# Graph attention layer: one gathered step in 26 is fetched row by row from the queues of SyncE and ScalarE

## The reference

```python
h = jnp.maximum(_layernorm(x, axis=-1), 0.0)
h = (h @ W_node.T).reshape(num_nodes, H, HD)
e = (edge_features @ W_edge.T).reshape(num_edges, H, HD)
att = jnp.sum(jnp.concatenate([h[src], h[tgt], e], axis=-1) * a, axis=-1)
att = jnp.where(att > 0, att, 0.2 * att)
m = jnp.maximum(segment_max(att, tgt), 0.0)
ex = jnp.exp(att - m[tgt])
denom = segment_sum(ex, tgt) + (num_edges - deg)[:, None] * jnp.exp(-m)
x = x + segment_sum((ex / denom[tgt])[:, :, None] * h[src], tgt).reshape(num_nodes, H * HD)
```

## Time and profile before

| | us |
|---|---|
| median of 3 runs | 4519.24 (4519.19 to 4522.25) |
| the profiled execution, its own time | 4519.71 |
| its span in the profile | 4517.7 |
| POOL busy | 3382.6 (75%) |
| DVE busy | 2492.8 (55%) |
| ACT busy | 1366.4 (30%) |
| PE busy | 819.8 (18%) |
| mean DMA rate | 139 GB/s |

### The profile page before, as it was taken

How to read it: one execution, slowest core, us unless ns; L and a number is a source line. 1 busy time by engine, 2 the same in 40 slices (tenths; PEclk the granted TensorE clock), 3 DMA queues, 4 the chain that set the end, 5 groups by cost and what they waited for, 6 DMA issues and landing times.

```text
span 4517.7 us, 21382 instructions
## 1 busy us (share of the span) xinstructions
PE 819.8 (18%) x3685; PEld 777.8 (17%) x3685; DVE 2492.8 (55%) x3230; ACT 1366.4 (30%) x1008; POOL 3382.6 (75%) x3532
## 2 busy tenths in 40 slices
PE   6301111112121211111121212121111112121200
PEld 4301111111111111111111111111111111111100
DVE  7516555555555555555555555555555555555553
ACT  8103333333333333333333333333333333333320
POOL 6777777777777777777777777777777777777756
PEclk6655555555555555555555555555555555555555
DMA  7424444444444444444444444444444444444453
GB/s 265 131 90 136 138 134 141 130 141 135 142 135 142 135 142 135 138 139 132 138 134 142 135 142 135 142 134 142 135 134 140 130 141 135 142 135 142 134 171 97
DMA packets 189542, 627.98 MB, mean 139 GB/s; under 512 B 74865, under 2 KB 75634, under 8 KB 188882
## 3 DMA queue, kind: packets, MB, share of 16 engines
q0 software_dynamic: 115936, 252.37, 23.3%
q1 hardware_dynamic: 73586, 375.40, 22.5%
HBM read 382.66 MB, written 244.86 MB: 139 GB/s over the span
## 4 chain that ended last, share of the span: by engine, by line
POOL 72%; issue 24%; DMA 1%; DVE 1%; PE 0%; POOLq 0%; ACT 0%; DVEq 0%; SPq 0%; ACTq 0%
POOL slots L291 70%; POOL tdst_scratch L294 1%; DMA V<-in_dst_dram,chunk_i 1%; POOL V L291 1%; DVE pen L448 1%; PE ae L721 0%; DVE slots L463 0%; POOL rstd L304 0%; POOLq L173 0%; DVE V L571 0%; ACT pen L364 0%; DMA rows_scratch<-slots 0%; DMA state_scratch<-R 0%; POOLq L332 0%; DVE V L581 0%
## 5 line engine op out<-in xcount | busy, mean ns | idle before, releaser
L291 POOL DMA_INDIRECT slots<-rows_scratch,idx x3224 | 3076.0, 954 | 982.4 <-issue 982.4
L732 PE MATMUL ae<-w_att,eab 128*128 128x8 f32 x3224 | 707.0, 361 | 3375.0 <-DVE z L550 3373.2
L732 PEld LDWEIGHTS ae<-w_att,eab 128*128 128x128 f32 x3224 | 696.3, 331 | 3385.8 <-DVE z L550 2433.3
L581 DVE TENSOR_TENSOR_SCAN V<-A,V 128x1848 f32<-128x1848 f32 x248 | 993.6, 4007 | 18.1
L401 ACT ACTIVATE A<-D 128x1848 f32<-128x1848 f32 x248 | 425.1, 1714 | 1849.3 <-DVE V L581 1849.3
L545 DVE TENSOR_TENSOR z<-slots,big 128x52 f32<-128x52 f32 x248 | 62.3, 251 | 1567.4 <-DMA slots<-rows_scratch,idx 1567.4
L412 ACT COPY R<-V 128x1768 f32<-128x1768 f32 x248 | 791.1, 3190 | 2.8 <-DVE V L581 2.8
L571 DVE TENSOR_TENSOR V<-slots,wexp 128x1716 f32<-128x1716 f32 x124 | 401.6, 3239 | 13.8
L571 DVE TENSOR_TENSOR V<-slots,extra 128x1716 f32<-128x1716 f32 x124 | 400.5, 3230 | 13.7
L399 ACT ACTIVATE wexp<-D 128x52 f32<-128x52 f32 x124 | 27.0, 218 | 562.5 <-DVEq L566 562.5
L399 ACT ACTIVATE extra<-D 128x52 f32<-128x52 f32 x124 | 27.0, 218 | 475.4 <-DVEq L566 475.4
(11 more groups left out here) (148 smaller groups left out, 535.2 us busy)
## 6 DMA issues: line engine op xcount, KB each, us to landing
state_scratch<-R SPq DMA_DIRECT2D x248, 884.0 KB, 4.2
eab<-in_ea_dram SPq DMA_DIRECT2D x126, 832.0 KB, 6.3
slots<-rows_scratch,idx POOLq DMA_INDIRECT x3224, 2.6
rows_scratch<-slots SPq DMA_DIRECT2D x14, 476.0 KB, 2.5
tdst_scratch<-eab SPq DMA_DIRECT2D x4, 1612.0 KB, 30.9
big<-tdst_scratch SPq DMA_DIRECT2D x8, 806.0 KB, 10.9
big<-in_x_t_dram SPq DMA_DIRECT2D x14, 448.0 KB, 8.3
big<-in_x_dram SPq DMA_DIRECT2D x7, 896.0 KB, 11.8
```

The lines of the kernel that those rows point to most:

```text
L291: pool.indirect_dma_start(buf, None, table, bass.IndirectOffsetOnAxis(ap=index, axis=0)).then_inc(done, 16)
L581: nc.vector.tensor_tensor_scan(V[:, k, 0:VAL * COL], a_all, V[:, k, 0:VAL * COL], 0.0, ALU.mult, ALU.add).then_inc(scanned, 1)
L732: last = mm(ps_ae[k][:, n * 2 * H:(n + 1) * 2 * H], eab[:, k, n * P:(n + 1) * P], w_att[:, :], start=True, stop=True)
```

## The change

In blocks with odd `q` POOL issues 12 gathers instead of 13. The 13th step's 128 rows are fetched by 128 DMAs of one row each: SP issues those for partitions 0 to 63 and ACT those for partitions 64 to 127. The node numbers lie in a new input `single`, of which a stretch for four blocks at a time is in `sidx` on one partition. An engine reads 16 of them into registers, issues 16 DMAs whose source address is worked out from a register, and so on four times. That is done for block `i + 2` in the body of block `i`, at its end: on SP after the store of block `i - 1`, on ACT after the copy of block `i - 1`; both wait for `val_done` of block `i - 2` before. Each block of the eight has a semaphore for either half, and DVE waits for both before L545. The rows for block 1 are fetched before the loop. The last body fetches rows that no block uses, and POOL waits for them before its final gathers.

```diff
+KP = KB - 1
+SPN = 64
+ACN = P - SPN
+        sidx = sb("sidx", [1, 2, SLOTS * P], i32)
+        def single_rows(eng, q, p0, n, done):
+            half, base = q // SLOTS, q % SLOTS * P
+            for a in range(p0, p0 + n, 16):
+                _, at = nc.values_load_multi_w_load_instructions(
+                    sidx[0:1, half, base + a:base + a + 16], engines=(eng.engine,), min_val=0, max_val=NP - 1,
+                    skip_runtime_bounds_check_because="node numbers of the input")
+                for j in range(16):
+                    eng.dma_start(slots[a + j:a + j + 1, q % SLOTS * KB + KP, :], rows[ds(at[j], 1), :]).then_inc(done, 16)
...
         @block.sync
+            single_rows(sp, 1, 0, SPN, row_dma_sp[1])
...
                 if not (isinstance(i, int) and i == 0):
                     store(i - 1, 1 - q % 2)
+                ahead(it, q)
+
+            def ahead(it, q):
+                a = (q + 2) % UN
+                if a % SLOTS == 0:
+                    sp.wait_ge(sidx_dma[a // SLOTS], it * 16 + (16 if q + 2 < UN else 32))
+                    sp.sem_inc(sp_rows, 1)
+                if q % 2:
+                    after(sp, val_done, it * UN + q - 1)
+                    sp.sem_inc(sp_rows, 1)
+                    single_rows(sp, a, 0, SPN, row_dma_sp[a])
+                if a % SLOTS == SLOTS - 1:
+                    sp.wait_ge(sidx_taken, it * UN + q + 1)
+                    sp.dma_start(sidx[:, a // SLOTS, :],
+                                 single[:, ds((it * 2 + (q + 2) // SLOTS) * (SLOTS * P) + 2 * SLOTS * P, SLOTS * P)]).then_inc(sidx_dma[a // SLOTS], 16)
...
         @block.gpsimd
-                for j in range(KB):
+                for j in range(KB if q % 2 == 0 else KP):
...
+            pool.wait_ge(row_dma_sp[1], (ITERS + 1) * 16 * SPN)
+            pool.wait_ge(row_dma_act[1], (ITERS + 1) * 16 * ACN)
...
         @block.scalar
                 if not (isinstance(i, int) and i == 0):
                     copy_state(i - 1, 1 - v, it, q)
+                a = (q + 2) % UN
...
+                if q % 2:
+                    after(act, val_done, i - 1)
+                    act.sem_inc(act_rows, 1)
+                    single_rows(act, a, SPN, ACN, row_dma_act[a])
+                act.sem_inc(sidx_taken, 1)
...
+            single_rows(act, 1, SPN, ACN, row_dma_act[1])
             loop(act, body)
...
         @block.vector
-                dve.wait_ge(gather_dma[s], it * (32 * KB) + 16 * KB * (q // SLOTS + 1))
+                n = KB if q % 2 == 0 else KP
+                dve.wait_ge(gather_dma[s], it * (32 * n) + 16 * n * (q // SLOTS + 1))
+                if q % 2:
+                    dve.sem_inc(block_begun, 1)
+                    dve.wait_ge(row_dma_sp[q], it * (16 * SPN) + 16 * SPN)
+                    dve.sem_inc(block_begun, 1)
+                    dve.wait_ge(row_dma_act[q], it * (16 * ACN) + 16 * ACN)
```

More of the change, by code:

```diff
@@ L32, with graph_attention_kernel @@
 RING = 8
+KP = KB - 1
+SPN = 64
+ACN = P - SPN
 PIECES = 8
 PT = T // PIECES
-def graph_attention_kernel(nc, x, x_t, src, dstf, dst16, lasts, ends, first, ea, w_node, w_node_t, a_blk, we2,
+def graph_attention_kernel(nc, x, x_t, src, dstf, dst16, lasts, ends, first, single, ea, w_node, w_node_t, a_blk, we2,
                            ident_c, centre_c, cols_c, out):
@@ L156, in graph_attention_kernel @@
         gather_dma = [sem(f"gather_dma{k}") for k in range(SLOTS)]
+        sidx_dma = [sem(f"sidx_dma{k}") for k in range(2)]
+        row_dma_sp = [sem(f"row_dma_sp{k}") for k in range(UN)]
+        row_dma_act = [sem(f"row_dma_act{k}") for k in range(UN)]
+        sidx_taken = sem("sidx_taken")
         store_dma = [sem(f"store_dma{k}") for k in range(2)]
@@ L164, in graph_attention_kernel @@
         get_dma = [sem(f"get_dma{k}") for k in range(STEPS)]
-        slots_taken = sem("slots_taken")
+        slots_taken, block_begun, act_rows, sp_rows = sem("slots_taken"), sem("block_begun"), sem("act_rows"), sem("sp_rows")
         em_done, group_done, stored = sem("em_done"), sem("group_done"), sem("stored")
@@ L239, in _ @@
             sp.dma_start(idx[:, 0, :], src[:, 0:SLOTS * KB]).then_inc(idx_dma[0], 16)
+            for k in range(2):
+                sp.dma_start(sidx[:, k, :], single[:, k * SLOTS * P:(k + 1) * SLOTS * P]).then_inc(sidx_dma[k], 16)
             for g in range(STEPS):
@@ L253, in _ @@
                 sp.dma_start(big[:, a:b], td_rows[:, a:b]).then_inc(td_dma[k], 16)
+            for k in range(2):
+                sp.wait_ge(rows_stored[k], 16 * (STEPS // 2))
+                sp.wait_ge(sidx_dma[k], 16)
+            single_rows(sp, 1, 0, SPN, row_dma_sp[1])
             state_rows = state_d[0:P * T, :].rearrange("(p t) r -> p (t r)", p=P)
@@ L264, in body @@
                     j = it * 2 + q // SLOTS
-                    after(sp, gather_dma[SLOTS - 1], j * (16 * KB))
+                    after(sp, gather_dma[SLOTS - 1], j * (16 * KP))
                     sp.dma_start(idx[:, 1 - q // SLOTS, :], src[:, ds(j * (SLOTS * KB) + SLOTS * KB, SLOTS * KB)]).then_inc(idx_dma[1 - q // SLOTS], 16)
@@ L272, in body @@
                     store(i - 1, 1 - q % 2)
+                ahead(it, q)
[12 more added lines that the diff above has]
+                                 single[:, ds((it * 2 + (q + 2) // SLOTS) * (SLOTS * P) + 2 * SLOTS * P, SLOTS * P)]).then_inc(sidx_dma[a // SLOTS], 16)
             loop(sp, body)
             store(EB - 1, 1)
+            for k in range(2):
+                sp.wait_ge(sidx_dma[k], (ITERS + 1) * 16)
             sp.wait_ge(d_ready, EB)
@@ L405, in body @@
                     copy_state(i - 1, 1 - v, it, q)
+                a = (q + 2) % UN
+                if a % SLOTS == 0:
+                    act.wait_ge(sidx_dma[a // SLOTS], it * 16 + (16 if q + 2 < UN else 32))
+                    act.sem_inc(act_rows, 1)
+                if q % 2:
+                    after(act, val_done, i - 1)
+                    act.sem_inc(act_rows, 1)
+                    single_rows(act, a, SPN, ACN, row_dma_act[a])
+                act.sem_inc(sidx_taken, 1)
             def copy_state(b, k, it, q):
@@ L412, in copy_state @@
                 nc.scalar.copy(R[:, k, :, :], vcols(k)[:, :, 1:COL].rearrange("p c t -> p t c")).then_inc(copied, 1)
+            for k in range(2):
+                act.wait_ge(rows_stored[k], 16 * (STEPS // 2))
+                act.wait_ge(sidx_dma[k], 16)
+            single_rows(act, 1, SPN, ACN, row_dma_act[1])
             loop(act, body)
@@ L777 @@
     ends[:-1, 3] = dst2[1:, 0]
+    single = _np.zeros((1, (BLOCKS + 3 * SLOTS) * P), _np.int32)
+    single[0, :BLOCKS * P] = srcp.reshape(P, BLOCKS, KB)[:, :, KB - 1].T.reshape(-1)
     eap = _np.zeros((P * T, K), f4)
@@ L791 @@
         "x": xp, "x_t": xt, "src": _np.concatenate([srcp.reshape(P, T), _np.zeros((P, SLOTS * KB), _np.int32)], axis=1), "dstf": dst2.astype(f4), "dst16": dst512.astype(_np.int16),
-        "lasts": dst512[:, -1].astype(f4).reshape(1, CL), "ends": ends, "first": dst2[:, 0:1], "ea": eat,
+        "lasts": dst512[:, -1].astype(f4).reshape(1, CL), "ends": ends, "first": dst2[:, 0:1], "single": single, "ea": eat,
         "w_node": w_node, "w_node_t": w_node.T, "a_blk": a_blk, "we2": _np.concatenate([w_edge, w_edge], axis=1),
```

## The result

The changed kernel took 6686.39 us (median of 4 runs, 6685.77 to 6698.24), the kernel before 4519.22 beside it: 1.480 times as long, 95% interval 1.4774 to 1.4825. That is 2,167 us slower. The forecast was 8,400 with a range of 6,200 to 10,500, so the side and the mechanism held and the size was 1,714 us off. L186 is the register load and L190 the row's DMA.

What follows compares the result with a forecast made beforehand. POOL bounded the kernel before, SP's ring the changed one: 355.6 us to the first scan, 123 pairs of 63.9, 58 at the end, 142 of tail and 2 around make 8417, stated as 8,400; range 6,200 to 10,500.

Steps and rivals of the forecast that it cites:

- the ring: Scan to scan through SP's queue, per pair of blocks: 5.4 + 46.4 + 2.3 + 9.8 = 63.9 us.
- The price of a row: On SP's and ACT's queues: 0.60 us per single-row DMA with address work, 38.4 us for 64.
- cheap row: Rival on the queues: a single row issues in 0.15 us, 46 us a pair, 6,200 us in all; chance 0.11.
- The register reads: Node numbers read into registers on either queue: 0.125 us each, 8 us for 64.
- The landing: After SP's last row is issued, before L545: 2.3 us until it has landed.
- What isn't rows: In SP's ring: 5.4 us from scan to the end of the store, 9.8 from L545 to the next scan's end.
- The start: Block 1's rows land at 341.8 us instead of L545 at 324.5; its scan ends at 355.6.
- the end: From the last odd ring's scan until POOL may start its final gathers: 58 us instead of 16.5.
- ACT just covered: ACT's queue is through 51.8 us after the scan, 2.3 us before SP's rows have landed.
- One generator: Rival: both queues' DMA issues exclude each other, 80.5 us a pair, 10,500 us in all; chance 0.15.
- The dear row: Rival on the queues: a single row costs 1.5 us, 121.5 us a pair, 15,600 us in all; chance 0.09.
- the hidden rows: Rival: SP's stretch fits beside POOL's gathers at 0.22 us a row, POOL stays the bound, 4,375 us; chance 0.03.

Runs made afterwards that it cites:

- SP's rows alone: ACT's 64 rows of each odd block left out of the changed kernel, SP's kept; 6695.8 us.
- The probe: The kernel before with DMAs of 1 to 128 rows and register loads added at its end to read issue lengths, on another chip; 5178.28 us, second version 5194.07.
- Experiments two and three: Two: SP's 64 rows left out of the changed kernel, 6196.7 us. Three: SP issues its rows ahead of the store in the changed kernel, 6230.53 us.
- rows in four pieces: The changed kernel with constant row addresses and each row's DMA cut into four separate pieces of 32 floats, on another chip; 10290.17 us.
- the constant rows: The changed kernel with all 128 single-row DMAs at constant addresses, without register loads and address work; 5701.26 us.
- the eight pieces: The changed kernel with constant row addresses and each row's DMA written as 8 x 17 floats, on another chip; 7271.7 us.

## Why the prediction was right, and where its size was off

**The bound moves from POOL to SP's queue.** As forecast. The forecast had the ring of scan, store, SP's rows, landing, L545, scan; rows and chain show it link by link, and SP's rows alone give 6,696 us. POOL's 156 us of saved work are lost in 2,268 us of waiting for slots. The count fell to 3,100. POOL is busy for 49% of the span; "under half" holds only just, and would have been some 39% of 8,400.

**The price of a row is the term that was off.** The prediction said that "the issue is a fixed cost that hardly knows the size: a row of 544 bytes should not come cheaper", and took 0.60 us for a row with its address work. It is 0.41: the issue is 0.225 and not 0.35 to 0.43. By the prediction's own list that is a sign of being wrong, "an issue that is much shorter", and the time lies near the low end of its range: 6,450 stood for 0.48 us a row with its read, and it is 0.52. The rows that misled were all of 128 partitions, first_i with its 0.5 KB too; they showed that the bytes don't matter and were read as if the partitions didn't either. The probe tells the two apart: 0.25 for one partition, 0.35 to 0.43 for 128. The "cheap row" rival named this gap, and assumed 0.15 for the issue. 64 x 0.19 = 12.2 us a pair too much. zero_row's 1.32 us was no price of a row, as the prediction had read it.

**The register reads** were put at 64 x 0.125 = 8.0 us; four loads of 16 took 2.58 + 3 x 1.23 = 6.3, 1.7 less. That the size was nearly right is luck, as the picture was wrong: there are no 64 reads but four, each mostly cheaper by the register than one alone, and the one right behind the store is twice as long. The Trainium skill (Runtime: NRT & Kernel Launch, Instruction fetch mechanics) has about 200 ns a register; here 1.23 / 16 = 0.08 in a load of sixteen and 0.48 in a load of one, so the measured numbers decide.

**The landing** was put at 2.3 us and is 1.0 to 1.2 from the last issue, 1.1 less. **What isn't rows**, 5.4 and 9.8 us, was read from the profile of before and came out at 5.5 and 9.8.

**Together** the three are 12.2 + 1.7 + 1.1 = 15.0 us a pair, 63.9 - 15.0 = 48.9 against 50.05 measured; the 1.1 that are too much are the 0.7 at the first rows of each load and small gaps. (63.9 - 50.05) x 123 = 1,704 us. The start was 15 us too late, the end 13 us too long, for the same reason, and the tail right: 8,417 - 1,704 - 28 = 6,685. (The terms that the prediction names for the end, 5.4 + 46.4 + 4, give 56 and not 58.)

**ACT just covered.** As said: its copy of the even block ends at 3083.5, 3.2 us before SP's rows have landed, where 2.3 was forecast; its own terms, 0.2 + 1.7 + 3.2, add up to 5.1 and not 5.4, which makes it 2.6. Experiments two and three show that this cover is what it looked like: with SP's ring opened the time falls by 456 us only, to the one that ACT sets.

**One generator.** Refuted as it was put, a row of each queue in 0.86 us. Where ACT issues beside SP, rows of SP start 0.41 us apart, and where it no longer does as well; without ACT's rows the issue is still 225 ns. The Trainium skill (Perfetto Trace Analysis, DMA Instruction — HWDGE) has a lock on a shared generator; at one row in 0.41 us on each queue no run here shows a wait for it. With rows in four pieces, 0.55 us alone and 0.69 beside the other queue, something is shared; that it is this lock is not shown.

**The dear row and the hidden rows.** Neither. Hidden rows needed 0.22 us a row with its read, and it is 33.2 / 64 = 0.52. Even with constant addresses it is 0.32, and then the landings lag.

## What to carry to other kernels

A gather of 128 rows costs POOL 1.26 us; the same rows as single DMAs cost two queues 33 us each. Before giving a queue small work, multiply: instructions per item, their gaps, and what stands on the queue behind them; then ask which wait the stretch starts from, since a ring that starts at the last scan gives it no room however idle the queue looks. Read a cost from the row that is like it in the dimension that counts, and where the trace has only one shape (here 128 partitions) keep the range open to the cheaper one.

## What the runs showed of the hardware

- A DMA issue on SP is 0.25 us for 1 or 2 partitions, 0.30 for 8, 0.42 for 16 and 32, 0.60 for 64, 0.35 to 0.43 for 128, with 512 bytes each; for one row with the address in a register it is 0.225 on SP and 0.213 on ACT. The 0.60 is unexplained.
- A row in four separate pieces takes 0.55 us of SP's queue to issue while ACT's issues nothing, and 0.69 beside ACT's.
- A register load right behind the issue of the 884 KB store takes 2.6 to 2.85 us instead of 1.23, with ACT's rows or without them.
- Single rows from both queues, issued as fast as one in 0.15 us, landed at one in 0.25 us in the mean (32.2 us for 128), while the DMA engines together were busy for under a third of the time. That they share one DMA engine is argued, not shown.
- On two other chips, instructions of SP, ACT and PE come 0.70 us apart for stretches, and the kernel before takes 5,153 us instead of 4,519. Of the kernels here it hits the one with many small instructions harder: before takes 1.14 times as long there, the constant rows 1.28 times (5,701 us, and 7,272 with the eight pieces, which make the same packets).
